# Twelve short matmuls on ones into the free bank ahead of the transposes of the later norms and of the heads' outputs

## What is computed

```python
x = x + attn_a(layernorm(x))   # 16 heads of 16, softmax over 1024 tokens, q/k/v/o with LoRA (rank 16)
x = x + ffn(layernorm(x))      # ternary weights, 256 -> 1024, gelu, 1024 -> 256
x = x + attn_b(layernorm(x))   # see below
x = x + ffn(layernorm(x))      # the same ternary weights
```

## Time and profile before

| | us |
|---|---|
| median of 3 runs | 355.96 |
| lowest, highest | 355.44, 357.6 |
| the profiled execution | 356.57 |
| its span, first to last instruction | 354.8 |
| mean granted TensorE clock in it | 0.976 |

### The profile page before, as it was taken

The page is one execution under the profiler, slowest core; times in us unless marked ns, Lnnn a source line. Parts: engine busy times, 40 slices in busy tenths (PEclk is TensorE's granted clock), DMA queues, the critical chain, the costliest instruction groups (busy, mean ns, idle before and its releaser), DMA issues.

```text
span 354.8 us, 5514 instructions
## 1 busy us (share of the span) xinstructions
PE 328.0 (92%) x1909; PEld 147.0 (41%) x1909; DVE 281.7 (79%) x471; ACT 264.0 (74%) x465; POOL 128.7 (36%) x133
## 2 busy tenths in 40 slices
PE   7999787999989999999999999999998957979796
PEld 2653442222222222222222234438745723647685
DVE  6456999799989999999999543517959998899774
ACT  1575114799989999999999977996479442577694
POOL 5042019999100000000005000400499976995030
PEclk9999997899999999999999999999999996999899
DMA  7936962353340000000000000000000000000011
GB/s 225 309 62 116 155 165 48 66 127 69 59 91 0 3 0 3 0 1 2 0 3 1 3 0 1 2 0 2 0 3 0 1 0 2 0 0 2 1 61 59
DMA packets 14814, 14.57 MB, mean 41 GB/s; under 512 B 4995, under 2 KB 13126, under 8 KB 14598
## 3 DMA queue, kind: packets, MB, share of 16 engines
q1 hardware_dynamic: 12358, 12.09, 14.9%
q10 hardware_dynamic: 2176, 1.64, 1.5%
q0 software_dynamic: 256, 0.52, 0.9%
HBM read 5.78 MB, written 1.05 MB: 19 GB/s over the span
## 4 chain that ended last, share of the span: by engine, by line
PE 63%; DVE 12%; SPq 10%; ACT 7%; issue 4%; DMA 2%; POOL 2%; ACTq 0%; DVEq 0%; POOLq 0%
PE ps L1417 14%; PE ps L1403 12%; SPq L535 8%; PE ps L1557 6%; PE ps L1545 6%; PE ps L1380 5%; PE ps L1332 4%; DVE mx L1095 3%; PE ps L1530 3%; PE ps L1589 2%; PE ps L1362 2%; DMA pack<-m_rows 1%; ACT ps L929 1%; PE ps L1300 1%; DVE s_wide L1202 1%
## 5 line engine op out<-in xcount | busy, mean ns | idle before, releaser
L888 ACT ACTIVATE pbuf<-ps,exp_scale 128x512 f32<-128x512 f32 x256 | 156.5, 693 | 13.7 <-PE ps L1403 10.9
L1095 DVE TENSOR_REDUCE mx<-ps 128x1 f32<-128x1024 f32 x128 | 150.4, 1219 | 11.1 <-PE ps L1380 8.1
L1403 PE MATMUL ps<-pack 64*128 64x512 f16 x256 | 87.9, 387 | 3.4 <-ACT pbuf L888 1.3
L1417 PE MATMUL ps<-pbuf,v_slot 128*32 128x512 f32 x512 | 68.8, 611 | 1.3 <-ACT parts L873 1.3
L1403 PEld LDWEIGHTS ps<-pack 64*128 64x128 f16 x256 | 23.1, 94 | 88.1 <-ACT pbuf L888 61.7
L1380 PE MATMUL ps<-pack 64*128 64x512 f16 x128 | 48.8, 385 | 4.8 <-DVE mx L1095 4.5
L1380 PE MATMUL ps<-parts,pack 64*128 64x512 f16 x128 | 49.9, 394 | 0.0
L750 POOL TENSOR_TENSOR pbuf<-wT 128x1024 f32<-128x1024 f32 (+3 forms) x32 | 48.2, 1534 | 3.5 <-ACT wT L958 3.4
L705 POOL COPY v_slot<-v_sb 128x512 f32<-128x512 f32 x8 | 4.9, 614 | 114.5 <-PE ps L1417 93.0
L681 POOL TENSOR_TENSOR rstd<-rstd,minus_half 128x2 f32<-128x2 f32 x16 | 11.4, 715 | 72.9 <-DVE rstd L1014 72.9
L1189 DVE SCALAR_TENSOR_TENSOR pack<-ps,g_unit,pack 128x512 f16<-128x512 f32 (+1 forms) x40 | 24.6, 639 | 14.1 <-ACT pack L941 14.1
(11 more groups left out here) (145 smaller groups left out, 392.7 us busy)
## 6 DMA issues: line engine op xcount, KB each, us to landing
w_nat<-in_L_ffn_w_dram SPq DMA_DIRECT2D x2, 1024.0 KB, 7.0
pack<-pack SPq DMA_DIRECT2D x3, 512.0 KB, 4.9
pack<-pbuf SPq DMA_DIRECT2D x20, 64.0 KB, 3.1
x_res<-in_L_attn_a_x_dram SPq DMA_DIRECT2D x4, 256.0 KB, 4.0
pack<-parts SPq DMA_DIRECT2D x16, 64.0 KB, 2.3
pack<-parts SPq DMA_DIRECT2D x32, 32.0 KB, 2.0
out_dram<-x_res SPq DMA_DIRECT2D x4, 256.0 KB, 2.1
w_nat<-in_L_attn_b_Wqkv_dram ACTq DMA_DIRECT2D x1, 768.0 KB, 6.7
```

The source lines that it names most:

```text
L888: act.activation(pbuf[:, c % 2, j, :], ps[:, b, :], ACT.Exp, scale=exp_scale[:, 0:1]).then_inc(drained[b], 1)
L1095: dve.tensor_reduce(mx[:, par, k:k + 1], ps[:, b:b + 2, :].rearrange("p b k -> p (b k)"), AX_X, ALU.max) \
L1403: pe.matmul(ps[:, b, :], k_group[0:ROWS, at, j, P * c:P * c + P].rearrange("p g t -> p (g t)"), q_rows[0:ROWS, at, qh, j, :].rearrange("p ...
L1417: ins = pe.matmul(ps[32 * j:32 * j + 32, PV_BANK, :], v_slot[:, qh, c, j, :], pbuf[:, c % 2, j, :], start=(c == 0), stop=(c == TT - 1))
```

## The change

`keep_busy(out, n)` issues `n` matmuls of 128 x 128 ones (bf16) by 128 columns of ones into the first 128 columns of the bank that the transposes behind it will overwrite. It is called with `n` = 12 in `transpose_pair` for `k` >= 2 (eight calls), ahead of the wait for the normalised pair, and in `o_to_features` for the second attention (eight calls), ahead of the wait for `("vs",t)`. For that, `to_fill` comes ahead of these waits.

```diff
--- before.py
+++ after.py
@@ -71,6 +71,7 @@
 
 PAIR_BANKS = (0, 2)
 WARM_UP = 17
+IDLE_FILL = 12
 SCORE_BANKS = (4, 5, 7)
 PV_BANK = 6
 SETUP_BANKS = (4, 5, 7, 6)
@@ -1308,9 +1309,16 @@
                 pe.matmul(out, ones[:, :], squares[:, m, 0:1], start=True, stop=False)
                 pe.matmul(out, ones[:, :], squares[:, m, 1:2], start=False, stop=True).then_inc(fill_sem(key), 1)
 
+            def keep_busy(out, n):
+
+                for _ in range(n):
+                    pe.matmul(out, onesb[:, 0:P], onesb[:, 0:P], start=True, stop=True)
+
             def transpose_pair(key):
                 _, k, p = key
                 n = number["norm", k, p]
+                if k >= 2:
+                    keep_busy(to_fill(pe, key)[:, 0:P], IDLE_FILL)
                 if k == 0:
                     pe.wait_ge(xn_ready, n + 1)
                 else:
@@ -1510,11 +1518,12 @@
             def o_to_features(key):
                 _, which, t = key
                 n = number[key]
+                out = to_fill(pe, key)
                 if which == "a":
                     is_drained(pe, ("ao_t", t))
                 else:
+                    keep_busy(out[:, 0:P], IDLE_FILL)
                     is_drained(pe, ("vs", t))
-                out = to_fill(pe, key)
                 for c in range(DC):
                     ins = pe.transpose(out[:, P * c:P * c + P], o_norm[:, n % 2, P * c:P * c + P], ident[:, :])
                 ins.then_inc(fill_sem(key), 1)
```

## The result

The changed kernel took 359.94 us, the median of 7 runs (359.31 to 361.02), where the kernel before took 356.25 beside it (7 runs, 355.44 to 357.95): a ratio of 1.0112, 95% interval 1.0082 to 1.0142. It is slower by about 1%. The profiled execution took 359.47 us, its span is 357.7, its mean granted clock 0.98. So it lies 2.90 us above the profiled execution before (356.57), and the medians lie 3.7 apart.

The account below looks back on a forecast made before the run. It took TensorE's waits and two late half-clock stretches as what could be won, against ten fills without cover. Delay of 3.4 us at h(1,0,0), plus 0.675 twice, less 1.7, is +3.0 on 356.57: 359.6 us, range 357.0 to 361.4.

Parts of the forecast that it names:

- The signs that it named: Expected in the later profile, including half clock at the first late dip and h(1,0,0) later by 1.5 us or more.
- The price of a fill: Twelve matmuls with weight loads on TensorE: 56 ns each, 0.675 us at full clock, 1.35 at half.
- Up to `("o","b",0)` and `("lnt",2,2)`: Three uncovered fills less 0.77 us cover: +1.26 us; fills of ("o","b",1) and ("lnt",2,2) lie in a 1.84 us wait.
- The bank wait: At ("o","b",2) and 3, fills start only after DVE drains the bank; the empty 1.99 us stays and the clock falls.
- The first low-clock stretch: From ("o","b",2) to ("lnt",2,3): clock falls again, two fills at half clock; +1.1 us, the middle of +0.7 and +1.55.
- the two guesses for the clock's return: After the first late fall: full clock back at 300.8 (+1.55 us) or at 299.1 (+0.7).
- The four fills in a row: ("lnt",2,3), ("o","b",4), ("lnt",3,0), ("lnt",3,1) in a full stream: +2.70 us, less 0.41 cover before DVE's second step.
- `("o","b",7)`, `("lnt",3,3)` and the second fall: Tail: two uncovered fills, +0.675 us each; the clock fall at 331.5 goes, -1.7 us.
- The sum: All terms together: 3.4 + 0.675 + 0.675 - 1.7 = +3.0 us on the profiled 356.57, giving 359.6 us.
- the first fall did not go: Rival: the clock fall at 294.4 to 300.8 goes too, -0.6 for +1.1 us; 357.9 us, chance 0.35.
- the second did not stay: Rival: the fall ahead of ("o","b",7) stays, so 1.7 us are not won; 361.3 us, chance 0.15.
- the fills were not free: Rival: TensorE has slack at the ten counted places, so only the clock gains stay; 353.1 us, chance 0.08.

Follow-up runs that it names:

- e4: Changed kernel with 24 matmuls instead of 12 at all sixteen places, in their own banks; 368.58 us, 1.0331 of the kernel before.
- e6: Changed kernel without the fills of ("o","b",1) and ("lnt",2,2); 357.37 us, 1.0047 of the kernel before.
- e1: Changed kernel with the fills of ("o","b",2) and ("o","b",3) put into the long-free bank of ("qk",5), not waiting for L1227; 357.61 us, 1.0036 of the kernel before.
- f13: Changed kernel without the two small DVE steps (GpSimd turns the mean, a TENSOR_REDUCE adds epsilon); 356.61 us, 1.0024 of the kernel before.
- e3: Kernel before plus twelve matmuls at each of eight places the prediction put on the path, none in a wait; 356.57 us, 1.0011 of the kernel before.
- f10: Kernel before, no fills, without the two small DVE steps (GpSimd turns the mean, a TENSOR_REDUCE adds epsilon); 355.87 us, 0.9987 of the kernel before.
- f11: n8 without the two small DVE steps (GpSimd turns the mean, a TENSOR_REDUCE adds epsilon); 352.87 us, 0.9905 of the kernel before.
- n9: n8 plus eight matmuls ahead of each maximum tile from 51 to 62 us; 355.97 us, 0.9986 of the kernel before.
- e2: Kernel before with fills only inside late waits: 12, 24, 12 and 6 matmuls at four places; 355.38 us, 0.9965 of the kernel before.
- n8: Kernel before with the late waits nearly filled: 22, 24, 30, 8, 22 and 7 matmuls at six places; 355.93 us, 0.9976 of the kernel before.

## Why the prediction was right, and where it was not

The forecast was 359.6 us and the median 359.94. The signs that it named came as well: the spacing of 56 ns, the fills of `("o","b",2)` and 3 behind L1227, half clock at the first place and full clock through `bo_y` 6 and 7, `h(1,0,0)` over 1.5 us late, and no wait ahead of `("o","b",7)`. Step by step, on the trace of the changed kernel, delays behind the common point:

- *The price of a fill.* 0.67 us for twelve in the chain at full clock (predicted 0.675), 1.20 and 1.46 at half (1.35). By the Trainium skill, "TensorE: Matmul & The Clock Gate", section "Back-to-back issue gap", a fill would be an estimated 0.97 us and the sum 3 us higher. The 0.67 us here and the 8.9 us that e4 adds disagree with it.
- *Up to `("o","b",0)` and `("lnt",2,2)`.* +1.18 there, predicted 1.26; e6 shows that the fills of `("o","b",1)` and `("lnt",2,2)` are covered.
- *The bank wait.* Right: the fill of `("o","b",2)` starts with DVE's L1227, 1.89 us empty ahead of it, and the clock falls.
- *The first low-clock stretch.* Mis-sized. The term was +1.1, between +0.7 and +1.55. With 303.15 - 302.34 less the 0.51 it measured +0.30. Of the two guesses for the clock's return, 299.1 was near (298.9 measured) and 300.8 was not; taking the middle cost 0.4. The rule behind 299.1, counted from the start of the dense work, would have given 299.5 with the start that was measured (296.04), so its hit is in part luck. The rest is that the work arrived 1.08 late rather than 1.26, and that the two fills took 1.25 each instead of 1.35.
- *The four fills in a row.* 63.42 - 60.75 = +2.67 at `h(1,0,0)`: 0.30 + 2.70 - 0.41 = 2.59. The cover of 0.41 was about right.
- *`("o","b",7)`, `("lnt",3,3)` and the second fall.* +3.44 and +2.38: one fill, then one fill less 1.7. The fall was gone, and e1, e4, e6 and f13, with the same fills there, lack it too, while e3, without them, has it. f10 lacks it without fills, after a fall 18 us earlier, so the fills are not the only thing that can keep it away.
- *The sum.* The change's own terms came to +2.38, not +3.0. What closed the gap in the profiled execution was 0.51 us from ahead of the change, which no term held and which is spread between executions. So the agreement to 0.3 us is partly luck. The medians lie 3.7 apart, and no run explains why they are 0.8 further apart than the two profiled executions.

The rivals: the first fall did not go, the second did not stay, and the fills were not free. What the prediction didn't see is that its terms hold for an execution with the clock of the two traces, and not for the mean of many. Eight fills cost 0.4 us by the ratio (e3) where the sum gave some 4, and 24 more matmuls in a covered place go with 2.3 us between the ratios (e6), while twice the fills cost about what the sum says (e4: 8.9 us between the last products, 7.8 by the ratios). Each fill costs its 0.675 where it is not covered, as the table shows at `("lnt",2,2)` and, for e3, between `("o","b",7)` and `("lnt",3,3)`. But the moment at which the clock falls moves as well, and with it whether DVE meets the stall. A fall ahead of 291 costs little, since TensorE has slack there (f10, low from 285.4 to 288.8, is at `("o","b",3)` 0.31 us ahead of f11, which had fills and no fall); one at 294 to 301 costs up to 2.4 us (e3 against before). That the fills are what moves it is argued, not shown. For the kernel before, the second profiled execution had each of its three falls 0.8 us later than the first. Its unprofiled runs spread over 352.95 to 360.14 us, with granted clocks of 0.952 (357.9 to 360.1 us) to 0.981 (353.0 to 356.7), mean 0.971. Both profiled executions of before had 0.976, the commonest value (31 of 85 runs) and a little above that mean. The runs of e3 had 0.980 in the mean. That the fills buy this higher clock fits all the numbers, but no run isolates it.

## What to carry to other kernels

Before filling a wait, look at what the wait is on: an instruction that needs the bank cannot start ahead of the signal that frees the bank, and then the fill is pure delay. Count the fills that have no wait ahead of them at full price, here ten of sixteen. A term for the clock read from one execution is one draw: ask what it would be if the fall came a few us earlier or later, and whether another engine (here DVE, standing for GpSimd) takes the won time before it reaches the end.

## What the runs showed of the hardware

A DVE instruction on 128x2 numbers can stand until an instruction of GpSimd ends. In the kernel before, DVE timeline and then GpSimd:

```profile
291.48 1.47 DVE L1013 TENSOR_SCALAR less_mean<-mv 128x2 f32<-128x2 f32 x1
...
304.07 0.17 DVE L1013 TENSOR_SCALAR less_mean<-mv 128x2 f32<-128x2 f32 x1
...
290.58 4.09 POOL L750 TENSOR_TENSOR pbuf<-wT 128x1024 f32<-128x1024 f32 x2 [1.87 <-ACT wT L958]
```

The price runs from nothing (0.17 us, in e3 at 292.01, 0.66 us ahead of GpSimd's start at 292.67) to 2.29 us (n9), by which of the two begins first. The Trainium skill, "SBUF — State Buffer", section "Who interferes with whom", says that the two engines share one pair of ports as an exclusive lock, that `tensor_scalar` can enter a mode that takes it, and that `tensor_reduce` never contends on trn2. This case's traces agree with both in their times (1.48 and 2.29 us against 0.16 us inside the product); in which mode the instruction was, none of them shows. It was in the trace of before, and on its last chain, and the prediction passed over it; since it took 1.46 us in the kernel after as well, it cancelled in the sum.

The clock's fall was the second surprise. In e2 it came at 284.4, in the kernel before at 294.0, though TensorE has the same instructions in both up to 291.9. In e2, TensorE had been at work without a wait for the 4 us ahead of it, on matmuls of 16 to 256 columns; in before it had stood for most of 4.6 us. With 24 matmuls in the two waits (e1) the fall came 2.7 us later than after, less than it differs between e2 and before, while 84 in the waits of 284 to 296 us (n8, n9, f11) went with no fall in that stretch, and so did the fills of f13. These are one profiled execution each, so none of it is a rule.
